# Sampling loops: the first operation of each round over both halves at once

## The reference, cut to what matters

```python
def corner(yi, xi, w):
    valid = (yi >= 0) & (yi < H) & (xi >= 0) & (xi < W)
    v = value[n_idx, clip(yi), clip(xi), g_idx]
    return v * (w * valid)[..., None]
sampled = (corner(y0, x0, (1 - wy) * (1 - wx)) + corner(y0, x0 + 1, (1 - wy) * wx)
           + corner(y0 + 1, x0, wy * (1 - wx)) + corner(y0 + 1, x0 + 1, wy * wx))
out = (sampled * mask[..., None]).sum(axis=4)
```

## Time and profile before

| what | before |
|---|---|
| time, median of 3 runs | 1047.3 us (1045.13 to 1049.42) |
| span of the profiled execution | 1044.4 us (its total isn't given) |
| TensorE busy | 931.1 us, 89% |
| VectorE busy | 888.4 us, 85% |
| ScalarE, GpSimd busy | 398.5 us, 165.2 us |
| products of the tap loops (128x512) | 516, mean 684 ns |
| products of the row loops (128x512) | 600, mean 678 ns |
| mean granted TensorE clock | 0.944 |

### The profile page before, as it was taken

The page is one execution under the profiler, slowest core; times in us unless marked ns, Lnnn a source line. Parts: engine busy times, 40 slices in busy tenths (PEclk is TensorE's granted clock), DMA queues, the critical chain, the costliest instruction groups (busy, mean ns, idle before and its releaser), DMA issues.

```text
span 1044.4 us, 23348 instructions
## 1 busy us (share of the span) xinstructions
PE 931.1 (89%) x5226; PEld 368.5 (35%) x5227; DVE 888.4 (85%) x1645; ACT 398.5 (38%) x540; POOL 165.2 (16%) x131
## 2 busy tenths in 40 slices
PE   3899779299999999999964999999999999999895
PEld 1435666133333323333241333233322332233353
DVE  3756656899999989989968899989998999899863
ACT  3533233481341472421145612661446016621031
POOL 6200000001302241301200022221222121412000
PEclk9899697699999999999995999999999999999987
DMA  7830000301110140110213001430022113501301
GB/s 145 295 121 1 1 1 2 85 2 45 45 46 23 46 111 14 32 46 23 49 26 80 23 23 45 100 78 22 24 76 57 34 34 71 130 2 43 68 1 42
DMA packets 37584, 55.15 MB, mean 53 GB/s; under 512 B 16971, under 2 KB 18323, under 8 KB 37396
## 3 DMA queue, kind: packets, MB, share of 16 engines
q1 hardware_dynamic: 35268, 42.28, 17.3%
q0 software_dynamic: 2256, 12.17, 3.4%
HBM read 41.02 MB, written 13.39 MB: 52 GB/s over the span
## 4 chain that ended last, share of the span: by engine, by line
PE 76%; DVE 8%; issue 5%; ACT 4%; DVEq 3%; DMA 2%; ACTq 1%; SPq 0%; POOL 0%; POOLq 0%
PE psA L1163 25%; PE T L1175 16%; PE psW L1175 14%; PE psA L741 7%; PE psA L1154 2%; DVE arena L1359 2%; ACT arena L1245 1%; PE psA L683 1%; DMA arena<-in_convw 1%; DMA arena<-planes 1%; PE T L689 1%; DVE arena L1526 1%; PE psA L696 1%; PE psA L972 1%; DVE arena L1344 1%
## 5 line engine op out<-in xcount | busy, mean ns | idle before, releaser
L1526 DVE TENSOR_TENSOR arena<-arena,psA 128x512 f32 x600 | 363.7, 678 | 6.2 <-PE psW L1175 2.9
L1499 DVE TENSOR_TENSOR arena<-arena 128x512 f32 x516 | 318.4, 684 | 29.8 <-issue 11.6
L1163 PE MATMUL psA<-arena,cst 64*64 64x512 f32 x2064 | 307.8, 607 | 2.3 <-DVE arena L1499 2.3
L1245 ACT ACTIVATE arena<-arena,cst (+2 forms) x212 | 150.0, 765 | 404.9 <-DVE arena L1499 390.1
L600 POOL TENSOR_TENSOR arena<-arena (+1 forms) x96 | 142.2, 1503 | 792.3 <-DVEq L1517 792.3
L1175 PE MATMUL psW<-arena,cst 128*64 128x512 f32 x632 | 191.7, 616 | 1.2 <-DVE arena L1526 1.2
L1175 PE MATMUL T<-arena,cst 128*64 128x512 f32 x568 | 171.7, 616 | 0.3 <-DVE arena L1526 0.3
L1163 PEld LDWEIGHTS psA<-arena,cst 64*64 64x64 f32 x2064 | 105.1, 131 | 178.8 <-issue 173.5
L1250 ACT ACTIVATE arena<-arena 128x1152 f32<-128x1152 f32 (+1 forms) x94 | 132.5, 1409 | 5.9
L1175 PEld LDWEIGHTS psW<-arena,cst 128*64 128x64 f32 x632 | 59.9, 135 | 131.2 <-DVE arena L1526 129.1
L1175 PEld LDWEIGHTS T<-arena,cst 128*64 128x64 f32 x568 | 54.0, 135 | 116.7 <-DVE arena L1526 115.2
(11 more groups left out here) (227 smaller groups left out, 571.6 us busy)
## 6 DMA issues: line engine op xcount, KB each, us to landing
arena<-planes SPq DMA_DIRECT2D x124, 284.0 KB, 4.1
planes<-arena POOLq DMA_DIRECT2D x1, 10000.0 KB, 29.3
planes<-arena SPq DMA_DIRECT2D x4, 512.0 KB, 5.3
arena<-in_convw POOLq DMA_DIRECT2D x4, 472.0 KB, 9.6
X<-in_x SPq DMA_DIRECT2D x8, 128.0 KB, 10.9
out_x<-X SPq DMA_DIRECT2D x16, 64.0 KB, 1.8
cst<-in_consts SPq DMA_DIRECT2D x1, 528.0 KB, 5.2
arena<-in_w SPq DMA_DIRECT2D x8, 64.0 KB
```

Of the source, the lines that this page charges most:

```text
L1163: mm = pe.matmul(psA[64 * h:64 * h + 64, at:at + BANK], ident[rows, rows], Pt[rows, i, h], start=False, stop=True, skip_group_check=True, ...
L1245: act.activation(dst[:, i], src, ACT.Abs, bias=column(i)).then_inc(hat_abs, 1)
L1499: dve.tensor_tensor(Pt[:, i, h].rearrange("p (s y) -> p s y", s=SPAN), along_y, along_x.broadcast_to([128, SPAN, HW]), ALU.mult)\
L1526: dve.tensor_tensor(Mt[:, i, h].rearrange("p (y c) -> p y c", c=CG), v.rearrange("p (y c) -> p y c", c=CG), w.rearrange("p (y c) -> p y c" ...
```

## The change

A round has three operations in place of four. The first covers both halves of `i` = 0 in one operation of 128x1024; the halves of `i` = 1 stay apart. The counters go up by three a round, and an operation waits for the one three before it. TensorE sums both halves of the first operation after one wait and signals once. The storage of `Pt` and `Mt` stays as it is, and so does the number of matmuls. The load of the unit's word on TensorE, and the register work on VectorE that stood after the first and the second product, now follow the first operation.

```diff
-LEAD = 4
+PARTS = [(0, 0, 2), (1, 0, 1), (1, 1, 2)]
+LEAD = len(PARTS)
...
 def sums(b, next_at):
-                    for i, h in itertools.product(range(2), range(2)):
-                        pe.wait_ge(p_ready, pe.snap(regs["taps"]) + (2 * i + h + 1))
+                    for part, (i, h0, h1) in enumerate(PARTS):
+                        pe.wait_ge(p_ready, pe.snap(regs["taps"]) + (part + 1))
                         pe.sem_inc(pe_turn, 1)
-                        for n in range(NI):
+                        for h, n in itertools.product(range(h0, h1), range(NI)):
...
                         mm.then_inc(w_sum, 1)
-                        if (i, h) == (0, 1):
+                        if part == 0:
                             unit_word(pe, regs, next_at)
-                    pe.reg_add(regs["taps"], regs["taps"], 4)
+                    pe.reg_add(regs["taps"], regs["taps"], LEAD)
...
 def accumulate(g, b):
+                    for part, (i, h0, h1) in enumerate(PARTS):
+                        pe.wait_ge(m_ready, pe.snap(regs["steps"]) + (part + 1))
+                        for h in range(h0, h1):
+                            mm = pe.matmul(acc_bank(g)[64 * h:64 * h + 64], const("stack"), Mt[:, i, h], start=False, stop=True,
+                                           skip_group_check=True, tile_position=(0, 64 * h))
+                        mm.then_inc(acc_sum, 1)
...
 def weights(b, rows_at, beside=None, at=None):
+                        dve.tensor_tensor(Pt[:, i, h0:h1].rearrange("p h (s y) -> p h s y", s=SPAN),
+                                          along_y.broadcast_to([128, h1 - h0, SPAN, HW]),
+                                          along_x.broadcast_to([128, h1 - h0, SPAN, HW]), ALU.mult)\
                             .wait_op(w_sum, regs["slots"], "sem-ge").then_inc(p_ready, 1)
...
 def weigh(b):
+                        dve.tensor_tensor(Mt[:, i, h0:h1].rearrange("p h (y c) -> p h y c", c=CG), v.rearrange("p h (y c) -> p h y c", c=CG),
+                                          w.rearrange("p h (y c) -> p h y c", c=1).broadcast_to([128, h1 - h0, HW, CG]), ALU.mult)\
                             .wait_op(acc_sum, regs["steps"], "sem-ge").then_inc(m_ready, 1)
```

More of the change, by code:

```diff
@@ L1165, in sums @@
                         mm.then_inc(w_sum, 1)
-                        if (i, h) == (0, 1):
+                        if part == 0:
                             unit_word(pe, regs, next_at)
-                    pe.reg_add(regs["taps"], regs["taps"], 4)
+                    pe.reg_add(regs["taps"], regs["taps"], LEAD)
             def accumulate(g, b):
                 with pe.Fori(0, pe.snap(regs[f"rows{b}"], min_val=1, max_val=SPAN // 2)):
[L1173 to L1177, removed]
+                    for part, (i, h0, h1) in enumerate(PARTS):
[4 more added lines that the diff above has]
+                        mm.then_inc(acc_sum, 1)
+                    pe.reg_add(regs["steps"], regs["steps"], LEAD)
             unit_word(pe, regs, 0)
@@ L1493, in weights @@
                 with dve.Fori(0, held_in(f"pairs{b}", 5, 1)):
-                    for i, h in itertools.product(range(2), range(2)):
-                        if h == 0:
+                    for part, (i, h0, h1) in enumerate(PARTS):
+                        if h0 == 0:
                             slot = held_in("second", 16 * K) * (HW // 16) if i else held_in("first", K - 1) * HW
[L1497 to L1500, removed]
+                        along_y = hys[i][:, bass.ds(rows_at, HY)].rearrange("p (h s t) -> p h s t", h=1, s=SPAN)[:, :, :, bass.ds(slot, HW)]
+                        along_x = axs[i][:, b, h0:h1, bass.ds(slot, HW)].rearrange("p h (s y) -> p h s y", s=1)
+                        dve.tensor_tensor(Pt[:, i, h0:h1].rearrange("p h (s y) -> p h s y", s=SPAN),
+                                          along_y.broadcast_to([128, h1 - h0, SPAN, HW]),
+                                          along_x.broadcast_to([128, h1 - h0, SPAN, HW]), ALU.mult)\
                             .wait_op(w_sum, regs["slots"], "sem-ge").then_inc(p_ready, 1)
-                        if (i, h) == (0, 0):
+                        if part == 0:
                             second_tap(b)
[L1504 to L1508, removed]
+                            if beside:
+                                beside()
+                            else:
+                                unit_word(dve, regs, at, "coming")
+                        elif part == 1:
                             dve.reg_alu(regs[f"list{b}"], regs[f"list{b}"], 8, op=ALU.logical_shift_right)
```

18 lines of the change are left out of this document (8 added, 10 removed).

## The result

The changed kernel takes 1051.6 us, the median of 6 runs (1051.40 to 1053.21); the kernel before, run beside it, 1046.4 us (6 runs). The ratio is 1.0057 with a 95% interval of 1.0046 to 1.0068: about 5 us slower, where 8 us slower was forecast. The profiled span grew from 1044.4 to 1049.5 us, at the same mean granted clock, 0.944. The sign came out as forecast. The reason for it did not, as the experiments show: what the forecast called the cause nets out to about nothing, and a collision between VectorE and GpSimd that the forecast left out makes the loss.

What follows compares the result with a forecast made beforehand. VectorE sets the pace, TensorE just behind. Steady taps +7.7, late taps +0.8, rows +7.4 and last rounds -7.8 make +8.1 us; added to the 1047.3 us median, 1055 us, range 1042 to 1068 us.

Steps and rivals of the forecast that it cites:

- The wide operation: VectorE's merged 128x1024 product takes 1.218 us (taps) or 1.212 us (rows), saving 0.067 us a merge.
- The rival of a dear row operation alone: Row loop's wide operation takes 1.282 us: near 1063 us; with dearer tap sums too 1073 us, together chance 0.17.
- A waits for its slot: A, a round's first operation, waits for TensorE to free its slot: tap rounds 0.18 us longer, row rounds 0.08 us.
- The second half's offset on TensorE: Summing the first operation's second half delays TensorE's freeing of the slot by 0.12 us (taps) or 0.10 us (rows).
- the second half costs nothing extra: Rival: TensorE sums the second half at no added time, -6.2 us, 1041 us; halfway 1047 to 1048 us; chance 0.27.
- Taps already late: 28 tap rounds already waiting for TensorE gain nothing and lose about 0.03 us each, +0.8 us.
- The last round of each loop: In 116 loops the last round, followed by another loop's slots, keeps the 0.067 us saving: -7.8 us.
- All lies on the path: The whole +8.1 us reaches the kernel's time, since VectorE is never far from busy in the loops.
- What lies beside: Register work, TensorE's list load and the second operation's sums stay covered, ScalarE absorbs little, SP's reloads keep their points.
- A page against this: Skill pages on larger operations favour the saving rival; advice to split VectorE instructions speaks against the change.
- Idle and busy time: Sign to look for: VectorE idle before its two product lines up about 27 us, busy time down some 19 us.
- the ring: Three slots in place of four delay rounds within loops: taps +7.7 and +0.8 us, rows +7.4 us.

Runs made afterwards that it cites:

- before_ring3: The kernel before with four narrow products, each waiting for the one three before it (LEAD = 3 in place of 4): 1158.8 us, 1.1060 of the kernel before.

## Why the forecast came out near, by its own steps

- **What bounds the kernel**: held. VectorE sets the pace and TensorE's return of A's slot is close behind.
- **The wide operation**: held. Forecast 1.218 us (taps) and 1.212 us (rows), measured 1.225 and 1.220 us as medians; the second operation starts 1.14 us after A in both, the third 1.74 us. The two halves aren't charged as two operations. (The rival of a dear row operation alone comes by its own terms to 18.7 us, 1066 us, not "near 1063"; nothing hangs on it.)
- **A waits for its slot**: held. 82 of 128 tap rounds start within 0.06 us of the sum that frees A's slot, all 71 that follow a round of their loop among them, and 96 of 149 row rounds; 70 and 90 were forecast. The restart after TensorE's end takes 0.047 us (0.045 forecast).
- **The second half's offset on TensorE**: mis-sized, 0.12 us (taps) and 0.10 us (rows) where 0.015 and 0.008 us were measured. TensorE frees A's slot 1.236 and 1.134 us after A's end; a narrow product's is 1.221 and 1.126 us. I had reasoned from fresh loads in the earlier trace rows and from the two halves of *two* operations in the earlier trace rows; the queued case that I had set aside, eight matmuls in 1.09 us, was the right row. So a tap round is 2.52 us, not 2.59, and a row round 2.40, not 2.47. The rows show it most: +0.5 us in place of +7.4 over 92 rounds. The taps came to +6.7 us in place of +7.7, over the 46 rounds that took under 2.45 us before: 42 of them lost 0.105 us each, and four lost 0.32 us or more to late sums. This is the rival "the second half costs nothing extra", with a price of -6.2 us, or 1047 to 1048 us "halfway there"; with GpSimd quiet the change is worth +0.2 us in the first convolution and -4.2 us in the second.
- **Taps already late**: forecast +0.8 us for 28 rounds, measured +0.5 us for 25.
- **The last round of each loop**: forecast -7.8 us, measured -1.0 - 4.1 - 4.5 = -9.6 us without the slow operations. A gap for register work ahead of some loops was hidden too.
- **"All lies on the path"**: not at the ends of spans. Where row loops of one round follow one another, value rows set the time (0.54 to 0.94 us of waiting before), and "the stall moves no transfer earlier" missed that a shorter loop would wait for them and a held-up one would not: -3.1 us.
- **"What lies beside"**: this is where the forecast failed. It went through VectorE's own queue, TensorE's load, ScalarE and SP, and never asked what GpSimd's mask products run beside, though they are the fifth group of the page it was read from, with a mean of 1503 ns. The term it lacks is +11.2 us, about 7.8 us net, as much as the whole sum.
- **"A page against this"**: the Trainium skill, Perfetto Trace Analysis, section "Optimizing Scalar/DVE Operations", gives its second advice, to split instructions, for engines that aren't saturated. VectorE was busy 24.71 of 25 us in the loops, so this advice had no bearing.
- **Idle and busy time**: forecast -19 us busy and +27 us idle; measured +2.6 and +3.0 us. A wait of 0.1 us a round mostly eats the 0.08 us by which operations overlap, which is not idle time, and the slow operations count as busy.

The account is then 6.7 + 0.5 + 0.5 - 9.6 - 3.1 + 11.2 = +6.2 us, +6.3 us before rounding, for a forecast of +8.1 us. The two numbers are close because two errors cancel: the ring and the last rounds together were put some 10 us too high (+8.1 against about -1.5), and GpSimd's net 7.8 us were missing. The forecast's direction was luck; its reason did not earn it.

What stays open: how much of before_ring3's loss at changes of loop is register work, and whether the remaining 8 or 9 slow operations can be avoided.

## What to carry to other kernels

When an edit shortens a loop, list every engine whose work runs beside that loop, and ask whether that work still fits; VectorE showed no contention here before the change, by a margin of about 0.1 us, while GpSimd's mean of 1503 ns against an undisturbed 1.42 us showed it. Then ask which operand pairs meet: here a VectorE product of two SBUF tiles and a GpSimd product block each other fully, while a row product with one operand in PSUM stayed at its usual 0.68 or 1.22 us beside GpSimd. And when a forecast comes out near, open the trace at the operations' extremes, not only at the means: the 14 slow operations that made the loss are a 1889 ns maximum beside an unchanged median of 684 ns.

## What the runs showed of the hardware that was not expected

- A tap product of two SBUF operands that a GpSimd product holds up (over 1.1 times its median) ends a fixed time after it, over all runs: 0.54 to 0.55 us for 148 narrow ones, 1.08 to 1.09 us for 24 wide ones. So its length depends on when it came, 0.81 to 1.91 us for 0.684 us and 1.43 to 2.18 us for 1.225 us. The 75 GpSimd products that came second end 1.26 to 1.28 us after the tap operation's end and take up to 1.96 us for 1.4 us. Row products with one operand in PSUM stay at 0.68 us.
- TensorE sums a wide operand's two halves, eight passes in four tiles, in 1.09 us, where four passes in two tiles take 1.07 us.
- A VectorE operation that waits for a semaphore holds back the register work behind it (it began 0.12 us after the operation's start, in place of 0.25 us before); one that is blocked by GpSimd does not hold back a go-ahead behind it, which came up to 4.67 us early.
- Three slots under four narrow products cost 112 us in before_ring3, where the slot's return alone was put at 15 to 20 us.
